# Row maxima of two units in one VectorE operation over two neighbouring PSUM banks, and preparation work moved between engines

## The reference

```
x = x + tanh(g_x) * attention(layernorm(x), ctx, ctx)
x = x + tanh(g_f) * ffn(layernorm(x))
attention: 32 query heads of width 16, 8 key/value heads (each used by 4 query heads),
           softmax(q k^T / 4) v per head, then Wfc and a bias
ffn:       silu(x Wg) * (x Wu) Wd with 2048 inner columns, plus a "routed" one with 256
           inner columns, scaled per token by softmax(top 2 logits) summed (the router)
```

## Time and profile before

| | |
|---|---|
| median of 3 runs | 882.84 us (882.19 to 884.73) |
| profiled execution, its own time | 885.25 us |
| its span | 883.5 us |
| PE busy | 861.7 us (98%) |
| DVE busy | 634.4 us (72%) |
| POOL busy | 478.8 us (54%) |
| ACT busy | 337.5 us (38%) |
| TensorE clock granted, mean | 0.994 of full |

### The profile page before, as it was taken

How to read it: one execution, slowest core, us unless ns; L and a number is a source line. 1 busy time by engine, 2 the same in 40 slices (tenths; PEclk the granted TensorE clock), 3 DMA queues, 4 the chain that set the end, 5 groups by cost and what they waited for, 6 DMA issues and landing times.

```text
span 883.5 us, 14905 instructions
## 1 busy us (share of the span) xinstructions
PE 861.7 (98%) x4929; PEld 641.5 (73%) x4929; DVE 634.4 (72%) x1085; ACT 337.5 (38%) x636; POOL 478.8 (54%) x485
## 2 busy tenths in 40 slices
PE   8988999999999899999999999999999999999998
PEld 6644555665665457888888888887788888888886
DVE  7889999889889956656556655679666566556565
ACT  4285686577667851122112211344221121112111
POOL 2312013002104999778668766854966696669640
PEclk9979999999999999999999999999999999999999
DMA  8652432432422112111111111212211121111102
GB/s 317 210 171 92 135 113 71 148 126 78 138 90 68 38 49 96 38 59 47 48 54 65 47 47 47 72 48 86 105 48 48 47 68 51 47 47 49 46 1 95
DMA packets 43611, 71.88 MB, mean 81 GB/s; under 512 B 6065, under 2 KB 21937, under 8 KB 43313
## 3 DMA queue, kind: packets, MB, share of 16 engines
q1 hardware_dynamic: 41984, 68.46, 24.1%
q10 hardware_dynamic: 1584, 2.88, 0.9%
HBM read 55.33 MB, written 15.73 MB: 80 GB/s over the span
## 4 chain that ended last, share of the span: by engine, by line
PE 83%; DVE 13%; issue 2%; ACT 1%; DMA 1%; SPq 0%; DVEq 0%; ACTq 0%
PE bank L1336 24%; PE bank L1338 23%; PE bank L1337 23%; DVE mcol L945 6%; PE bank L1421 4%; PE bank L1396 4%; PE bank L1411 2%; PE bank L1341 2%; DVE oN L1077 1%; DVE oB L1067 1%; DMA probs<-wv 1%; ACT probs L796 1%; DVE x_l L1299 1%; DVE aT L1082 0%; DVE aT_l L920 0%
## 5 line engine op out<-in xcount | busy, mean ns | idle before, releaser
L1336 PE MATMUL bank<-x_l,w_h 128*128 128x512 f32 x504 | 197.3, 391 | 0.3 <-DVE c L1159 0.2
L1337 PE MATMUL bank<-x_h,w_l 128*128 128x512 f32 x504 | 196.2, 389 | 0.0
L1338 PE MATMUL bank<-x_h,w_h 128*128 128x512 f32 x504 | 196.2, 389 | 0.0
L945 DVE TENSOR_REDUCE mcol<-bank 128x2 f32<-128x512 f32 x256 | 164.6, 672 | 21.3 <-PE bank L1396 21.1
L627 ACT ACTIVATE hT_h<-bank 128x512 fp32r<-128x512 f32 x72 | 43.2, 600 | 355.9 <-DVE bank L1274 347.2
L796 ACT ACTIVATE probs<-bank 128x512 f32<-128x512 f32 x256 | 138.9, 595 | 70.2 <-PE bank L1411 68.7
L579 POOL TENSOR_TENSOR w_l<-raw,w_h 128x512 fp32r<-128x512 f32 (+1 forms) x144 | 162.0, 1158 | 2.9
L1171 DVE SCALAR_TENSOR_TENSOR xa<-bank,tgf,xa 128x512 f32<-128x512 f32 x128 | 96.1, 751 | 77.7 <-PE bank L1338 77.6
L1336 PE MATMUL bank<-dn_l,hT_h 128*128 128x512 f32 x288 | 112.0, 389 | 0.0
L1337 PE MATMUL bank<-dn_h,hT_l 128*128 128x512 f32 x288 | 112.0, 389 | 0.0
L1338 PE MATMUL bank<-dn_h,hT_h 128*128 128x512 f32 x288 | 112.0, 389 | 0.0
(11 more groups left out here) (152 smaller groups left out, 1346.9 us busy)
## 6 DMA issues: line engine op xcount, KB each, us to landing
raw<-w_gu SPq DMA_DIRECT2D x36, 512.0 KB, 3.3
dnraw<-w_dn SPq DMA_DIRECT2D x36, 256.0 KB, 2.6
q_st<-q_scr SPq DMA_DIRECT2D x64, 128.0 KB, 2.6
q_st<-q_scr SPq DMA_DIRECT2D x64, 64.0 KB, 2.7
out<-xa SPq DMA_DIRECT2D x16, 256.0 KB, 2.0
cx_raw<-ctxT SPq DMA_DIRECT2D x12, 256.0 KB, 2.9
xa<-x SPq DMA_DIRECT2D x3, 1024.0 KB, 10.3
q_scr<-qx_h SPq DMA_DIRECT2D x12, 256.0 KB, 2.1
```

Source lines behind the costliest of these rows:

```text
L945: v.tensor_reduce(at[:, :, qt], sm_bank(n, s, u)[:, :].rearrange("p (r k) -> p r k", r=2), AX.X, ALU.max).then_inc(max_ok, 1)
L1336: mm(out, a_h, b_l, start=start, stop=False, skip_group_check=onto)
L1337: mm(out, a_l, b_h, start=False, stop=False, skip_group_check=onto)
L1338: return mm(out, a_h, b_h, start=False, stop=stop, skip_group_check=onto)
```

## The change

One DVE operation takes the maxima of both units of a pair, over a PSUM tensor of 1024 columns that covers two neighbouring banks (`twin`). Steps n < 2 use two such twins in turn; all later steps use `twin[0]` alone. So pair v of a later step waits until the maxima of pair v-1 are complete (`max_ok` at 8n + 2v, before 8n + 2v - 1). Beside it:

- `norm_rows(1)` and `(2)` become two GpSimd operations behind the root; `deviations(2)` moves from s = 4 to s = 5, behind `add_bias`.
- both `wfc_low` go from DVE in s = 2 and 3 to GpSimd before the loop, both `wfc_high` on ACT from s = 1 and 2 to before the loop; the Wfc DMA goes ahead of the first `put_max`, the x rows of the last block ahead of the loop.
- the router's weights are spread earlier on DVE, behind two `tile_stats`.
- `tile_stats` of the last block: one in each of s = 0, 2, 3, 4 at u = 6 instead of two in each of s = 2 and 3; `aggregates` at s = 5 instead of 4.
- `add_bias(0)` is cut in two around `cx_low(1, 2)` and `(1, 3)` on GpSimd.

```diff
+        twin = [psum_tensor(f"twin{i}", [P, 1024], f32) for i in range(2)]
+        bank = [twin[i // 2][:, i % 2 * 512:(i % 2 + 1) * 512] for i in range(4)]
-        def sm_bank(n, s, u):
-            return bank[u % 4] if isinstance(n, int) and n < 2 else bank[(0, 1, 5)[(UNITS * s + u) % 3]]
+        def sm_twin(n, v):
+            return twin[v % 2] if isinstance(n, int) and n < 2 else twin[0]
...
-            def maximum(n, s, u, par):
-                dve.wait_ge(sm_full[e], UNITS // 2 * n + u // 2 + 1)
-                v.tensor_reduce(at[:, :, qt], sm_bank(n, s, u)[:, :].rearrange("p (r k) -> p r k", r=2),
-                                AX.X, ALU.max).then_inc(max_ok, 1)
+            def maxima(n, w, par):
+                for e in range(2):
+                    dve.wait_ge(sm_full[e], UNITS // 2 * n + w + 1)
+                v.tensor_reduce(at, sm_twin(n, w)[:, :].rearrange("p (e r k) -> p e r k", e=2, r=2),
+                                AX.X, ALU.max).then_inc(max_ok, 2)
...
-                    pe.wait_ge(max_ok, UNITS * n + 2 * v - (0 if s == 0 and v == 0 else 1))
+                    pe.wait_ge(max_ok, UNITS * n + 2 * v)
...
                     for u in range(UNITS):
-                        if not last or s + 2 < STEPS:
-                            maximum(n + 2, (s + 2) % STEPS, u, s % 2)
+                        if u % 2 == 0 and (not last or s + 2 < STEPS):
+                            maxima(n + 2, u // 2, s % 2)
...
-                        if first and s in (2, 3) and u == 6:
-                            wfc_low(s - 2)
-                        if first and s in (2, 3) and u in (4, 7):
+                        if first and s in (0, 2, 3, 4) and u == 6:
                             dve.wait_ge(in_x[BLOCKS - 1], 16)
-                            tile_stats(T // P - TILES + 2 * (s - 2) + u // 7)
+                            tile_stats(T // P - TILES + max(s - 1, 0))
...
+                if lot > 0:     # GpSimd, in deviations
+                    g.tensor_scalar(nmr[:, 0, a:b], mv[:, 0, a:b, 0], -1.0, 0.0, ALU.mult, ALU.add).then_inc(neg_ok, 1)
+                    pool.wait_ge(rs_ok, lot + 1)
+                    pool.wait_ge(neg_ok, lot)
+                    g.tensor_tensor(nmr[:, 0, a:b], nmr[:, 0, a:b], rstd[:, 0, a:b], ALU.mult).then_inc(nm_ok, 1)
...
             deviations(1)
+            add_bias(0, 0, 2)
             cx_low(1, 2)
             cx_low(1, 3)
-            add_bias(0)
+            add_bias(0, 2, 4)
+            wfc_low(0)
+            wfc_low(1)
```

More of the change, by code:

```diff
@@ L151, in build @@
         raw, w_h, w_l = (raw0, raw1), (w_h0, w_h1), (w_l0, w_l1)
-        bank = [ctx.enter_context(nc.psum_tensor(f"bank{i}", [P, 512], f32)) for i in range(8)]
+        twin = [ctx.enter_context(nc.psum_tensor(f"twin{i}", [P, 1024], f32)) for i in range(2)]
+        bank = [twin[i // 2][:, i % 2 * 512:(i % 2 + 1) * 512] for i in range(4)]
+        bank += [ctx.enter_context(nc.psum_tensor(f"bank{i}", [P, 512], f32)) for i in range(4, 8)]
         STB, OTB, PJ = bank[2:4], bank[4], bank[6:8]
@@ L477, in _, with add_bias @@
             cx_low(1, 1)
-            def add_bias(tb):
+            def add_bias(tb, a=0, b=TILES):
                 pool.wait_ge(tb_ok, 1)
-                for j in range(TILES):
+                for j in range(a, b):
                     pool.wait_ge(xn_ok, TILES * tb + j + 1)
@@ L484, in add_bias, with wfc_low @@
                     g.tensor_tensor(tile, tile, tbias[:, :], ALU.add).then_inc(xb_ok, 1)
+            def wfc_low(half):
+                pool.wait_ge(w_hi, half + 2)
+                w = slice(half * DC * D // 2, (half + 1) * DC * D // 2)
+                g.tensor_tensor(wfc_l[:, :, :].rearrange("p c n -> p (c n)")[:, w], wfc_raw[:, w],
+                                wfc_h[:, :, :].rearrange("p c n -> p (c n)")[:, w].bitcast(f32),
+                                ALU.subtract).then_inc(wfc_ok, 1)
             deviations(1)
+            add_bias(0, 0, 2)
             cx_low(1, 2)
             cx_low(1, 3)
-            add_bias(0)
+            add_bias(0, 2, 4)
+            wfc_low(0)
+            wfc_low(1)
             def body(t, first, last):
@@ L498, in body @@
                         cx_low(t + 1, s)
-                    if first and s == 4:
-                        deviations(2)
                     if s == 4:
                         add_bias(t + 1)
+                    if first and s == 5:
+                        deviations(2)
             blocks(pool, body)
@@ L751, in _ @@
             cx_high(1, 2)
+            cx_high(1, 3)
             m_copy(0)
-            cx_high(1, 3)
+            wfc_high(0)
+            wfc_high(1)
             k_high(1)
@@ L800, in body @@
                             m_copy(n + 1)
+                        if u == 5 and first and s == 5:
+                            act.wait_ge(wfc_ok, 1)
                         if u == 5 and not (first and s == 0):
@@ L814, in body @@
                             continue
-                        if first and (s, u) in ((1, 1), (2, 1)):
-                            wfc_high(s - 1)
                         if s == 0 and u == 1:
@@ L996, in wq_low @@
                     wq_h[:, :, :].rearrange("p c n -> p (c n)")[:, w]).then_inc(wq_ok, 1)
[L998 to L1002, removed]
             v.memset(k_st[:, :, :, :].bitcast(f32), 1.0).then_inc(consts, 1)
@@ L1030, in _ @@
                 tile_stats(i)
+            v.memset(wr[:, :, :], 0.0).then_inc(wr_ok, 1)
+            dve.wait_ge(in_vectors, 64)
+            dve.wait_ge(wr_ok, 1)
+            v.tensor_copy(wr[:, :, 0:EXPERTS], wr_raw[:, :].rearrange("p (c e) -> p c e", c=DC)).then_inc(wr_ok, 1)
             q_low(0, 0)
@@ L1043, in _ @@
             aggregates(2)
-            for u in range(UNITS):
-                maximum(0, 0, u, 0)
-                if u == 1:
+            for w in range(UNITS // 2):
+                maxima(0, w, 0)
+                if w == 0:
                     q_low(0, 3)
[L1048 to L1053, removed]
+            for w in range(UNITS // 2):
+                maxima(1, w, 1)
             def a_low(n, c, bb):
@@ L1096, in body @@
                             x_low(nx, 2 * s - 1)
-                        if first and s in (2, 3) and u == 6:
-                            wfc_low(s - 2)
-                        if first and s in (2, 3) and u in (4, 7):
+                        if first and s in (0, 2, 3, 4) and u == 6:
                             dve.wait_ge(in_x[BLOCKS - 1], 16)
-                            tile_stats(T // P - TILES + 2 * (s - 2) + u // 7)
-                        if first and s == 4 and u == 0:
+                            tile_stats(T // P - TILES + max(s - 1, 0))
+                        if first and s == 5 and u == 0:
                             aggregates(BLOCKS - 1)
-                        if first and s == 5 and u == 0:
-                            norm_rows(2)
                         if prev:
@@ L1115, in body @@
                             if u == 7:
+                                if first and s == 5:
+                                    dve.wait_ge(wfc_ok, 2)
                                 a_low(n - 1, (s - 1) % CHUNKS, (s - 1) % STEPS // CHUNKS)
@@ L1395, in sm_pair @@
                         rows = slice(e * ROWS, e * ROWS + SM)
-                        last = mm(sm_bank(n, s, 2 * v + e)[:, j * S:(j + 1) * S],
+                        last = mm(sm_twin(n, v)[:, e * 2 * S + j * S:e * 2 * S + (j + 1) * S],
                                   q_st[rows, c, 2 * half + j, qt * P:(qt + 1) * P], k_st[rows, bb, c, :],
```

14 lines of the change are left out of this document (7 added, 7 removed).

## The result

The changed kernel takes **901.25 us** (median; 900.12 to 904.46) against 883.46 us before on the same chip: ratio 1.0209, interval 1.0191 to 1.0227. It is slower, as forecast (887.7 us), but by 17.8 us and not by 4.9; the time lies above the range. The profiled execution has a span of 898.1 us against 883.5, so 14.6 us are to be found in the trace.

A forecast was written before the change was run, and what follows sets the result against it. PE bounds the FFN and blocks 1 and 2; DVE and PE alternate in the first and last blocks. 5.5 + 0 - 2.7 + 2.1 = +4.9 us takes the median from 882.84 to 887.7 us; 8-in-10 range 881.5 to 892.

The forecast's parts named there:

- blocks 1 and 2: Middle attention blocks: PE waits 0.14 us more twice a step, extra in steps 1 and 2; +5.5 us for both.
- block 0 from its third step: First attention block: removed stalls offset by longer waits for whole pairs; 0 us, bounds -1.8 and +1.
- the loop's start: 44.5 to 62.9 us: PE's 1.9 us gap goes and two steps run at full clock; -2.7 us, bounds -1 and -4.
- the last block: Last attention block: look-ahead pairs, f_sum and a stretched divide cost more than merging returns; +2.1 us, 0 to +3.5.
- The distance over one pair: SM pair to next over probability matmuls: start 0.53, operation 1.22, answer 0.05, sum 1.80 us against 1.66.
- The account of steps 1 and 2: In blocks 1 and 2, pair 2 runs late in VectorE's order: step 1 costs +0.62 us, step 2 some +0.44.
- if Wfc landed late: Loop's start: a late Wfc transfer would make k_high(1) on ACT late by as much; bound +1 us.
- The clock: Loop's start: clock 0.72 today, falling to 0.50 behind PE's gap; forecast at 1.00 from 48 to 60 us.
- The third rival: Merged maximum costs as much as two, 0.1 us more at some 56 places, clock falls anyway; about 892 us, chance 0.12.
- Steps with q_low: Block 0, q_low before pair 2: PE waits for the whole pair, +0.54 us, step 8.10 to about 8.68 us.
- The rival "as much as two operations": Merged maximum takes 1.29 to 1.39 us, clock falls anyway; +10.5 us at worst, about 892 us, chance 0.12.
- The rival of a larger gain at the start: Loop's start gains 4 us, waits cost less, distance under about 1.70 us; -3.0 us, 879.8 us, chance 0.16.

The follow-up runs named there:

- e5: Changed kernel with one semaphore for both units of a pair and the pair's maxima raising their own by one instead of two; 895.79 us, ratio 1.0151.
- e1: Changed kernel with both units of a pair raising one semaphore, so the maxima wait for one count instead of two; 898.57 us, ratio 1.0168.
- e2: Changed kernel with single-unit maxima and the three banks of before, all moves of work kept; 883.97 us, ratio 0.9997.
- e7: e2 with SP issuing the q writes before the k reads in s = 4 of block 0; 881.64 us, ratio 0.9980.
- e12: The kernel of e7 measured once more without any edit, in five rounds; 881.51 us, ratio 0.9973.
- the best form of the moves: e9 with the low halves of Wfc back on VectorE, at u = 6 of steps 2 and 3; 881.00 us, ratio 0.9967.
- e9: e7 with ScalarE's Wfc splits back in steps 1 and 2 instead of before the loop; 882.53 us, ratio 0.9985.
- e10: e5 with the q write ahead of the k reads and ScalarE's Wfc splits back in steps 1 and 2; 896.45 us, ratio 1.0148.

## Why the prediction was wrong

The forecast for the trace, term by term, against the changed kernel and against e5, which is the changed kernel without the separate wait instruction (us, differences to the kernel before):

| term | forecast | changed | e5 |
|---|---|---|---|
| blocks 1 and 2 | +5.5 | +9.7 | +6.7 |
| block 0 from its third step | 0 | +2.8 | +1.2 |
| the loop's start | -2.7 | -1.5 | +0.6 |
| the last block | +2.1 | +3.6 | +1.9 |
| sum | +4.9 | +14.6 | +10.4 |

The e5 figure of the last block goes to its last SM pair; 0.4 us of its span lie behind that.

**The distance over one pair (0.53 + 1.22 + 0.05).** This is the step that failed first. Two of its terms stood: 1.22 (measured 1.217 mean) and 0.05. The start did not: 0.67 to 0.74 us. I took the 0.53 of an operation that waits for one semaphore and raises by one; the new one waits for two and raises by two, and then a separate wait instruction runs on VectorE's queue after the pair is full. I read its two waits as free because both units fill together. e5 prices it: 901.25 - 895.79 = 5.5 us. The last 0.04 us (0.57 against 0.53) is the second unit. The trace's semaphore records in blocks 1 and 2 show the first unit full 0.516 us after PE's first load and the second 0.550 us, before the change and after. VectorE starts 0.024 us behind the first of them before, and 0.023 us behind the second in e5; in e1 it is some 0.09 us behind it and in the changed kernel 0.12 to 0.19 us. "At nearly the same time" was 0.034 us, which at 16 places a block is some 0.5 us.

**Blocks 1 and 2, +5.5 us.** Measured +9.7. Without the wait instruction the two blocks of e5 last 153.3 against 146.6 us: +6.7, near my sum and the second unit's 0.034 us. The account of steps 1 and 2 was right: in e5 the pair after the late one starts 7.04 us into step 1, the 7.04 of the forecast, and the steps cost 0.6 and 0.4 us. The mechanism was right, and the term mis-sized through the distance. (I counted 1.66 to 1.68 us in 30 of 32 places; it is 29. The fourth step of a block differs in the kernel before itself, 8.63 us in block 1 and 7.96 in block 2.)

**The last block, +2.1 us.** Measured +3.6 in the changed kernel. Its look-ahead part, from the first to the last SM pair, lasts 51.7 us against 47.8, and 49.7 in e5: +1.9 there, near the forecast.

**Block 0 and the loop's start, 0 and -2.7 us.** This is the second step that failed; it makes 4.0 us of the 9.7 by which the trace misses the forecast (a part of the 4.0 is again the wait instruction). VectorE's stall of PE did not go but was split: in the place of one gap of 1.9 us PE has one of 1.28 us for the maxima and one of 0.71 us for ScalarE. What I had as a bound of +1 ("if Wfc landed late") was the case: ScalarE waited 2.88 us, so its first exponentials came 1.0 us later than before instead of earlier. And I looked for users of the moved work, not for what the faster steps would run into: the q write that lands late in step 5 (10.0 us there, 8.1 before). Both are transfers that the old, slower steps had hidden. The longer distances of the pairs do the rest.

**The clock.** That it stayed at 1.00 in the changed kernel was luck of the execution that was profiled: the other three show a mean of 0.997, 0.996 and 0.992, and the profiles of e1, e2, e5, e7 and e12, which have the same moves, fall to 0.50 at 47 to 50 us for 3.4 to 6.8 us. The fall of 10 us in the kernel before, which the earlier trace rows show, belongs to few executions. Its profiled one has a mean of 0.994. Of the 70 that ran beside the experiments 5 have 0.994 or 0.995 (median 885.45 us), 36 have 0.996 to 0.998 and 29 have 0.999 or 1.000 (median 882.97). So most of what a clock at full could give at the start was already in the median that I subtracted it from.

**Slips in the sums.** 18.4 - 7.8 - 8.2 - 0.3 is 2.1, not 2.3, and 8.10 + 0.54 is 8.64, not 8.68. The third rival's +10.5 makes 893.3 us, not 892. None of it decides the case.

**Steps with q_low, +0.54.** In the changed kernel the distance from the third to the fourth pair in such a step is 2.38 to 2.39 us, against 1.79 in the earlier trace rows: +0.6, of which 0.1 is the wait instruction (2.28 in e5, +0.5). Right. Such a step lasts 8.77 us in e5, where I had 8.68, and 9.02 in the changed kernel.

**Rivals.** The rival "as much as two operations" had the time nearest to the result, 892, for a cause that did not occur. The rival of a larger gain at the start (879.8 us) did not occur either: the distance it wanted under 1.70 us was 1.95 to 2.02, and even without the twins the best form of the moves comes to 881.0 us.

The range failed since I bounded the operation (1.14 to 1.39 us) and not its start. An upper bound of 0.15 us more on that, at some 60 places, would have moved the upper end from 892 to about 901.

## What to carry to other kernels

Merging two operations that drain a buffer saves one fixed part (0.07 us here). Taking away the spare buffer puts start, merged operation and answer (0.57 + 1.22 + 0.05 us) in PE's way at each turn, where 1.66 us of other work stands against it; compare these two before anything else, and let PE keep a bank to write while VectorE reads. When an edit changes how an operation waits and signals, price the wait instruction too: look whether the operation now waits on two semaphores or raises by more than one. Work moved to an idle engine must be checked in that engine's order for what it waits on, and against the two-input work of its neighbour at that moment; and steps that become faster bring transfers into view that they had hidden. Before a term is read from one profile, look whether its execution is like the others: its time against the median, its clock against theirs.

## What the runs showed of the hardware

- In these kernels a maximum on VectorE with one wait and an increment of one has no separate wait instruction, and starts 0.023 us after the last semaphore that it needs. With an increment of 2 the wait became an instruction of its own (21 ns, start 0.63 us after PE's first load of the pair), with two semaphores one of 50 ns (0.67 us), with a third wait beside the two 0.74 us; with one semaphore and an increment of 1, 0.57 to 0.58 us.
- A 128x1024 maximum over two neighbouring PSUM banks takes 1.217 us, two of 128x512 one behind the other 1.28. If reading on into the second bank costs anything, it is less than the fixed part that merging saves.
- A 128x256 product of VectorE with both inputs in SBUF lasts 0.40 to 0.43 us alone and 1.24, 1.72 or 2.20 us beside GpSimd's two-input subtraction of Wfc (e9 and e10), and ends 0.27 to 0.28 us after it in all three. Maxima from PSUM in the same stretch keep their 0.63 to 0.69 us. Not every meeting does this: at 219.43 us of the kernel before the product takes 0.41 us beside an addition of GpSimd's that had begun 0.02 us earlier. What decides it isn't shown.
- The granted clock of attention falls to 0.50, the 1.2 GHz level, for 3 to 10 us at a time. The length of the last gap of PE doesn't decide it. It fell behind gaps of 1.9 us (before the change), 1.8 us (e10) and 1.3 us (e9), and in e2 at 48.5 us with no gap over 0.54 us in the four us before it. It stayed at 1.00 behind gaps of 1.4 us in the changed kernel and 1.5 us at 322 us in e1. What decides it isn't shown. The stretches of e2:

```profile
46.00:48.00 2.00, 1.37 (x9) 0.76 (x10) 2.00 (x5) 2.00 (x5) 2.00 (x2) 1.00 1.07 354
48.00:50.00 2.00, 2.00 (x18) 1.17 (x21) 1.29 (x3) 2.00 (x6) 2.00 (x2) 0.62 0.98 131
50.00:52.00 2.00, 2.00 (x22) 0.96 (x14) 1.07 (x2) 0.95 (x2) 1.36 (x2) 0.52 0.15 15
```

- Profiles of one kernel differ: step 0 of the kernel of e7 took 9.09 us in one profile and 10.28 in the other, where their times are 881.94 and 882.06 us.
